# Layer pipeline on one core: TensorE's transposes and scores of a step set side by side, and all engines' operations reordered

## The reference, cut to what matters

```python
for i in range(DEPTH):                       # DEPTH = 6
    x = attn_layer(shift_tokens(x), Wqkv[i], q_scale[i], k_scale[i], Wo[i]) + x
    x = ffn_layer(shift_tokens(x), ln_g[i], ln_b[i], W1[i], b1[i], W2[i], b2[i]) + x
...
# attn_layer: 16 heads of 64, window 32 with one window of look-back
q = l2norm(q) * qs; k = l2norm(k) * ksc      # then rotary tables on both
sim = einsum('bhwie,bhwje->bhwij', bq, bk2) * 8.0; softmax over 64 keys; @ v; @ Wo
# ffn_layer: layer norm, a * gelu(gate) with 341 hidden features, W2
```

## Time and profile before

| | us |
|---|---|
| median of 3 runs | 1506.65 (1505.9 to 1509.11) |
| the profiled execution, its own time | 1507.59 |
| its span, first to last instruction | 1505.8 |
| TensorE busy / VectorE / GpSimd / ScalarE | 1441.7 / 1327.1 / 1209.8 / 1162.2 |

### The profile page before, as it was taken

How to read it: one execution, slowest core, us unless ns; L and a number is a source line. 1 busy time by engine, 2 the same in 40 slices (tenths; PEclk the granted TensorE clock), 3 DMA queues, 4 the chain that set the end, 5 groups by cost and what they waited for, 6 DMA issues and landing times.

```text
span 1505.8 us, 74802 instructions
## 1 busy us (share of the span) xinstructions
PE 1441.7 (96%) x32904; PEld 785.9 (52%) x32904; DVE 1327.1 (88%) x1789; ACT 1162.2 (77%) x2289; POOL 1209.8 (80%) x1051
## 2 busy tenths in 40 slices
PE   6877999999999999999999999999999999999985
PEld 6823444545545545545545545545555545545553
DVE  5478999989999989999999999989999999999974
ACT  4337888878888788888888888888888788888871
POOL 5148999878888888888888888888888888888841
PEclk9968999999999999999999999999999999999998
DMA  5100000020000020000020000020000000000000
GB/s 206 30 1 30 3 10 10 3 66 10 4 20 15 4 66 10 3 20 15 3 66 10 4 19 15 4 66 10 3 20 15 4 10 10 4 20 15 4 17 29
DMA packets 24564, 32.93 MB, mean 22 GB/s; under 512 B 2372, under 2 KB 21424, under 8 KB 23344
## 3 DMA queue, kind: packets, MB, share of 16 engines
q1 hardware_dynamic: 24240, 28.15, 5.8%
HBM read 20.80 MB, written 1.05 MB: 15 GB/s over the span
## 4 chain that ended last, share of the span: by engine, by line
PE 89%; DVE 5%; issue 2%; POOL 2%; ACT 1%; DMA 1%; SPq 0%; POOLq 0%; DVEq 0%; ACTq 0%
PE psq L257 22%; PE ring L279 21%; PE ring L309 11%; PE pss L298 9%; PE ring L267 9%; PE ring L323 8%; PE ring L333 4%; PE ring L346 1%; DVE qa L825 1%; PE ring L382 1%; DVE qb L841 1%; DVE mx L983 1%; DVE qb L961 1%; DMA xf<-x 0%; DMA mh<-in_bv 0%
## 5 line engine op out<-in xcount | busy, mean ns | idle before, releaser
L279 PE MATMUL ring<-mh,x0S 128*32 128x512 f32 x3072 | 407.9, 595 | 0.0
L257 PE MATMUL psq<-wqk,x0S 128*32 128x512 f32 x3072 | 394.9, 612 | 5.9 <-ACT sq L1200 4.9
L1332 POOL TENSOR_TENSOR qa<-qa,qb 128x1024 f32<-128x1024 f32 x96 | 229.2, 2388 | 6.7 <-DVE qb L961 6.7
L1391 POOL TENSOR_TENSOR qa<-qa,qb 128x1024 f32<-128x1024 f32 x96 | 228.6, 2382 | 0.0
L309 PEld LDWEIGHTS ring<-u,pT 128*32 128x32 f32 x6144 | 171.4, 111 | 61.8 <-issue 60.1
L309 PE MATMUL ring<-u,pT 128*32 128x128 f32 x6144 | 191.6, 274 | 4.1 <-DVE pT L978 4.1
L1373 POOL TENSOR_TENSOR pr<-pr,rden 128x1024 f32<-128x1024 f32 x96 | 183.9, 1916 | 12.8 <-DVE rden L860 12.8
L257 PEld LDWEIGHTS psq<-wqk,x0S 128*32 128x32 f32 x3072 | 93.6, 111 | 184.2 <-issue 168.4
L1352 POOL TENSOR_TENSOR qa<-qa,rn 128x1024 f32<-128x1024 f32 x96 | 182.7, 1903 | 0.2
L1368 POOL TENSOR_TENSOR qa<-qa,rn 128x1024 f32<-128x1024 f32 x96 | 182.8, 1904 | 0.0
L298 PEld LDWEIGHTS pss<-kT,qT 64*32 64x32 f32 x12288 | 134.8, 105 | 91.1 <-issue 83.6
(11 more groups left out here) (172 smaller groups left out, 2724.3 us busy)
## 6 DMA issues: line engine op xcount, KB each, us to landing
wqk<-in_wqk SPq DMA_DIRECT2D x6, 1024.0 KB, 8.6
mvT<-in_mvT SPq DMA_DIRECT2D x6, 512.0 KB, 3.8
wo<-in_wo SPq DMA_DIRECT2D x6, 512.0 KB, 5.2
xf<-x SPq DMA_DIRECT2D x24, 128.0 KB
xf<-x SPq DMA_DIRECT2D x24, 127.0 KB
rope<-in_rope SPq DMA_DIRECT2D x1, 2048.0 KB, 10.0
w<-in_w SPq DMA_DIRECT2D x6, 341.0 KB, 3.0
xmid<-in_x SPq DMA_DIRECT2D x4, 256.0 KB, 4.2
```

Source lines behind the costliest of these rows:

```text
L257: last = mm(psq[WIN * w:WIN * w + WIN, 512 * (n % 2):512 * (n % 2) + 512], x0S[:, tile * P + WIN * w:tile * P + WIN * w + WIN], wqk[:, l % ...
L279: last = mm(bank[WIN * g:WIN * g + WIN, :], x0S[:, tile * P + WIN * w:tile * P + WIN * w + WIN], mh[:, l % 2, g, :, :].rearrange("p j n -> ...
L1332: g_.tensor_tensor(qa[:, t % 2, 1024:2048], qa[:, t % 2, 1024:2048], qb[:, 1024:2048], ALU.add).then_inc(sum_k, 1)
L1391: g_.tensor_tensor(qa[:, t % 2, 0:1024], qa[:, t % 2, 0:1024], qb[:, 0:1024], ALU.add).then_inc(sum_q, 1)
```

## The change

Only orders and lags change; every operation, its operands, its semaphores and the waits in front of it stay as they are, but for the tile number that follows from the lag. In the table the tile numbers are those of step s; group operations, which stand in every fourth step, are in brackets with their lag.

| engine | before | after |
|---|---|---|
| TensorE | [G2 14], U3 s-5, U2 s-4, scores 1 s-4, q turn s-3, project q s-1, [A1 14], [F 12], mix 0 s-5, [G0 13], mix 1 s-5, [A0 13], U0 s-3, [Z 15], [A2 14], U1 s-3, [merge 8], [G1 13], project k s, [X 15], k turn s-2, scores 0 s-3 | [A2 15], mix 0 s-6, [G2 14], [G1 14], mix 1 s-6, U1 s-4, [X 16], U0 s-4, [A0 14], project k s-1, k turn s-3, q turn s-3, scores 0 s-4, scores 1 s-4, U2 s-4, U3 s-5, project q s-1, [F 12], [A1 14], [Z 15], [merge 8], [G0 13] |
| VectorE | subtract s-4, q product 1 s-1, [A1 14], q product 2 s-1, add x s-5, sum and reciprocal s-4, k squares' sum s-1, [A0 13], [statistics 9], [A2 14], [Z 15], q squares' sum s-1, k product 1 s, [aggregate 9], k product 2 s, small maximum s-1, transpose s-4, max s-3 | q squares' sum s-2, sum and reciprocal s-5, small maximum s-2, [A0 14], k product 1 s-1, k product 2 s-1, max s-4, transpose s-5, subtract s-4, q product 1 s-1, [statistics 9], q product 2 s-1, [Z 15], [aggregate 9], [A1 14], k squares' sum s-1, [A2 14], add x s-5 |
| ScalarE | [H 8], T0 and T1 s-2, [G2 13], U3 s-4, square k s, seed s-1, U2 s-3, T2 and T3 s-2, root's rest s-1, [F0 11], exp s-3, [G0 12], [F1 11], square q s, mask s-3, U0 s-2, U1 s-2, [xh 9], [G1 12], k look-back s-1, [X 14] | seed s-1, T0 and T1 s-2, root's rest s-1, square k s, T2 and T3 s-2, U2 s-3, U3 s-4, [xh 10], [F0, F1 11], exp s-3, [G0 12], [G2 12], [H 7], square q s, k look-back s-2, [G1 12], mask s-3, U1 s-2, [X 14], U0 s-2 |
| GpSimd | rb s-3, sum k s-2, rp and rn s-3, tables s, norm k s-3, norm q s-3, probabilities s-5, [group root 10], sum q s-2 | [group root 12], sum q s-4, rb s-4, probabilities s-7, tables s-2, rp and rn s-4, sum k s-3, norm q s-4, norm k s-4 |

The operations of the prologue's remainder move among these in the same way: the chunks' `chain_w` and `chain_d` now stand directly one behind the other, behind the k turn, behind U3 and at the end of the step, and the last `chain_d` of a step opens the next one. GpSimd's two layer norms of a unit go from lags 3 and 2 to 4. SyncE's program is not touched.

The core of the diff, TensorE's part:

```diff
             for s in range(STEPS + 20):
...
-                t = s - 4
-                if 0 <= t < STEPS:
-                    scores(t, 1).then_inc(s_ready, 1)
-                t = s - 3
-                if 0 <= t < STEPS:
-                    banks = [take("T2", t), take("T3", t)]
-                    pe.wait_ge(qn_q, t + 1)
-                    for bank, n in banks:
-                        wait(pe, freed[bank], n)
-                    turn([ring[bank] for bank, n in banks], t, 0)
...
-                t = s - 0
+                t = s - 1
                 if 0 <= t < STEPS:
...
                     wait(pe, sq_q, t)
                     project(t, 2)
                     project(t, 3).then_inc(pk_done, 1)
...
-                t = s - 2
+                t = s - 3
                 if 0 <= t < STEPS:
                     banks = [take("T0", t), take("T1", t)]
                     pe.wait_ge(qn_k, t + 1)
                     for bank, n in banks:
                         wait(pe, freed[bank], n)
                     turn([ring[bank] for bank, n in banks], t, 8)
...
                 t = s - 3
+                if 0 <= t < STEPS:
+                    banks = [take("T2", t), take("T3", t)]
+                    pe.wait_ge(qn_q, t + 1)
+                    for bank, n in banks:
+                        wait(pe, freed[bank], n)
+                    turn([ring[bank] for bank, n in banks], t, 0)
+                t = s - 4
                 if 0 <= t < STEPS:
...
                     pe.wait_ge(kprev_ready, t + 1)
                     scores(t, 0)
+                t = s - 4
+                if 0 <= t < STEPS:
+                    scores(t, 1).then_inc(s_ready, 1)
+                t = s - 4
+                if 0 <= t < STEPS:
+                    bank, n = take("U2", t)
+                    wait(pe, freed[bank], n)
+                    values(ring[bank], t, 2).then_inc(filled[bank], 1)
+                t = s - 5
+                if 0 <= t < STEPS:
+                    bank, n = take("U3", t)
+                    wait(pe, freed[bank], n)
+                    values(ring[bank], t, 3).then_inc(filled[bank], 1)
...
+                t = s - 1
+                if 0 <= t < STEPS:
+                    pe.wait_ge(sq_k, t + 1)
+                    project(t, 0)
+                    project(t, 1).then_inc(pq_done, 1)
```

More of the change, by code:

```diff
@@ L538, in _ @@
[L538 to L557, removed]
+                    hidden(ring[bank], 2, 0).then_inc(filled[bank], 1)
+                if chunk_at(s - 1, 0) >= 0:
+                    chain_d(chunk_at(s - 1, 0))
@@ new lines, in _ @@
+                if i >= 0:
+                    banks = [take("F0", i), take("F1", i)]
+                    pe.wait_ge(xh_ready, i + 1)
+                    for bank, n in banks:
+                        wait(pe, freed[bank], n)
+                    halves_turned([ring[bank] for bank, n in banks], lambda blk: xh[:, blk * P:blk * P + P], QUAD)
+                i = group_at(s, 14)
+                if i >= 0:
+                    bank, n = take("A1", i)
+                    wait(pe, freed[bank], n)
+                    hidden(ring[bank], 1, 0).then_inc(filled[bank], 1)
@@ new lines, in _ @@
+                i = group_at(s, 15)
+                if i >= 0:
+                    bank, n = take("Z", i)
+                    if i % GROUPS == 0:
+                        pe.wait_ge(w2_ready, 32 * (i // GROUPS + 1))
+                    abank, m = place["A2", i]
+                    pe.wait_ge(freed[abank], m + 1)
+                    wait(pe, freed[bank], n)
+                    narrow(ring[bank]).then_inc(filled[bank], 1)
+                i = group_at(s, 8)
+                if 0 <= i < LASTG:
+                    l, j = i // GROUPS + 1, i % GROUPS
+                    if j % 2 == 0:
+                        if j == 0:
+                            pe.wait_ge(mw_ready, 32 * (l + 1))
+                        merge((j, j + 1), l)
@@ new lines, in _ @@
+                i = group_at(s, 13)
+                if i >= 0:
+                    bank, n = take("G0", i)
+                    for r in range(2):
+                        nbank, m = place["F%d" % r, i]
+                        pe.wait_ge(freed[nbank], m + 1)
+                    if i % GROUPS == 0:
+                        pe.wait_ge(w1_ready, 16 * (i // GROUPS + 1))
+                    wait(pe, freed[bank], n)
+                    hidden(ring[bank], 0, 1).then_inc(filled[bank], 1)
+                if chunk_at(s - 1, 3) >= 0:
+                    chain_w(chunk_at(s - 1, 3))
@@ new lines, in _ @@
+                if chunk_at(s - 1, 1) >= 0:
+                    chain_W(chunk_at(s - 1, 1))
+                t = s - 5
+                if 0 <= t < STEPS:
+                    dve.wait_ge(p_ready, t + 1)
+                    if t >= 1:
+                        bank, n = place["Y", t - 1]
+                        dve.wait_ge(filled[bank], n + 1)
+                    v.transpose(pT[:, :, :].rearrange("p e n -> p (e n)"), pr[:, t % 2, :]).then_inc(pt_ready, 1)
+                if chunk_at(s - 1, 2) >= 0:
+                    chain_u(chunk_at(s - 1, 2))
@@ new lines, in _ @@
+                u = unit_at(s, 1)
+                if u >= 2:
+                    result(u)
+                if chunk_at(s, 0) >= 0:
+                    chain_u(chunk_at(s, 0))
+                i = group_at(s, 9)
+                if i >= 0:
+                    dve.wait_ge(bst_ready, i + 1)
+                    wait(dve, mrs_ready, i)
+                    for k in range(QUAD):
+                        last = v.bn_aggr(mv[:, k, :], bst[:, k, :])
+                    last.then_inc(mv_ready, 1)
```

664 lines of the change are left out of this document (302 added, 362 removed).

## The result

The change made the kernel slower: 1538.27 us (median of 4 runs, 1530.64 to 1550.14) against 1506.28 (4 runs, 1501.76 to 1509.11), a ratio of 1.0227 with an interval of 1.0164 to 1.029. The forecast was 1483, the range 1469 to 1500. The profiled execution took 1550.14 us, with a span of 1548.1.

The account below looks back on a forecast made before the run. TensorE's own matmul stream was taken as the bound: 35.5 us saved there less 12 us of new waits, 23.5 off 1507.59, gave 1484.1; with the profiled execution 0.9 above the median, 1483 us, range 1469 to 1500.

Parts of the forecast that it names:

- Nothing is added or left out on any queue: All queues: the change adds and removes no work, so TensorE alone comes out 35.5 us less.
- The three shape changes that fall away: TensorE's step: six changes of tile shape become three, saving 0.40 us a step, 38.4 us over 96 steps.
- The tight psq loop: Bank pair psq, shared by k and q: 0.37 us spare vanishes; rival that it takes most, 1492 to 1502, chance 0.20.
- My walk: Four-step count of TensorE and VectorE around psq: q projection waits 0.03, 0.14, 0.03 and 0.26 us, sum 0.46.
- classes 0 to 3: The four kinds of step by TensorE group work: F 0.53; G0, G2, G1, A0 3.44; A1, A2 1.72; Z, x transposes 3.17.
- ScalarE's squares as what is late next: q projection on psq: TensorE waits for ScalarE's squares, some 10 us in all; all waits together give back 12 us.
- VectorE at 90%: Sign of being right: VectorE's busy share near 90% of the span.
- GpSimd as the bound: Rival: both norm products, wanted at once, make the turns late; 1519 us at 0.5 us late a step, chance 0.07.
- The clock: Rival: turns and scores in one stretch drop TensorE to 1.2 GHz, 250 us more, 1756; chance 0.01.
- Joining the scores: TensorE: scores 1 directly behind scores 0 saves 0.13 us a step, taken between ends of 0 and 0.15.
- my sum: Whole kernel: 35.5 us gained on TensorE less 12 us of waits, 23.5 us off the profiled execution.
- costed the start at nothing within 3: Prologue and tail: lags tile against tile stay the same, so no cost, 3 us either way.

Follow-up runs that it names:

- aligned2: The changed kernel with 199 of its 576 projection and value parts run as two halves of 256 columns; 1498.96 us, 0.9945 against the kernel before.
- before_joined: The kernel before with one edit, scores 1 directly behind scores 0; 1533.06 us, 1.0193 against the kernel before.
- aligned: The changed kernel with 72 projection and value parts split into 256-column matmuls; 1505.67 us, 0.9994 against the kernel before.
- supply: The kernel before with 64 projection matmuls and four stretches of 1024 short matmuls behind its last TensorE instruction; ended 248 us after the kernel before.

## Why the prediction was wrong

**The step that failed** is "Nothing is added or left out on any queue", and behind it the sentence that TensorE works as long as its matmuls take. I counted the queues that the program writes and not the one that brings the program. The change adds no instruction, but it puts 320 of them into 2.6 us where before no block of 256 ran under 2.8. In the profiled execution the waits come to 53.5 us and the clock behind them to some 14 (before: 5.4 and 1.7), and no rival of mine contained it. The signs were there: half the scores take 0.79 us in the earlier trace rows, the page of before has the code queue, and its trace has three issue waits in the regular steps, all at a border.

**Point by point.**
- The three shape changes that fall away: right. The turns take 1.14 together, the q projection no longer has its 0.13, the scores 1.41 by the chain where I had 1.45. Their cover by other work held.
- The tight psq loop: right in size and kind. My walk had k to q at 6.20, 6.31, 6.20 and 6.43 in classes 0 to 3; in aligned2, where few stops are in the way, the medians from start to start are 6.18, 6.19, 6.18 and 6.42. From one k projection to the next, the shortest steps of the four classes in after are 11.92 (class 0), 14.87, 13.03 and 14.71 us, 54.5 together; my walk gave 11.92, 14.94, 13.11 and 14.79, together 54.8. In the kernel before they give 55.6.
- ScalarE's squares as what is late next: right in kind, too large in size, and not visible where I looked. I had forecast 12 us. The 3.7 us of waits of the psq matmuls for the squares belong to the early steps, and before has 5.2 of them, so they are no part of it. In the steady steps it is the weight load ahead of the matmuls that waits, as in the step of the chain above:

```profile
623.26 1.02 ACT L1117 ACTIVATE sq<-psq 128x1024 f32<-128x1024 f32 x1 [0.76 <-DVE qb L864]
...
624.34 0.16 PEld L257 LDWEIGHTS psq<-wqk,x0S 128*32 128x32 f32 x8 [0.78 <-ACT sq L1117]
624.34 1.92 PE L257 MATMUL psq<-wqk,x0S 128*32 128x512 f32 x16
```

  The squares end at 624.28, the first load goes at 624.34 and so no longer runs under the matmuls before it: the chain has 1.79 for this projection instead of 1.72. In 41 of the 43 steps of tiles 20 to 89 without a stop between k and q, the q projection starts within 0.15 us of the squares' end, and by the means of the four classes 0.03 to 0.08 us later behind the block ahead of it than where nothing holds it. At 0.06 in each of 96 steps that is an estimated 5 us.
- VectorE at 90%: wrong as a share (85%), because the span grew; its busy time fell from 1327.1 to 1313.3.
- GpSimd as the bound: the whole profile has one wait of a turn for it, of 0.3 us. The rival falls.
- The clock: I had named a granted clock under 0.97 as a sign of being wrong. It came at 0.972 (0.982 before), and the part that was lost was not lost by my route. Through turns and scores it stays at 1.00 (the window from 1186.60); it falls behind a stop. The Trainium skill (TensorE: Matmul & The Clock Gate, Part 4) has transposes not counting as activity; no run here shows the clock falling in the 1.14 us stretches of transposes alone.
- Joining the scores: my 0.13 can't be read alone. In the old order psq takes it back (before_joined); in the new one the whole step came out as summed.

The steps' gain is real, and aligned2 lets it be read: its profiled span is 16.4 us under that of before (1489.4 against 1505.8), where my sum had 23.5. The first scores start 2.3 us later (132.0 against 129.7), where I had costed the start at nothing within 3; from tile 0 to 20 it gains 10.0 (267.0 against 277.0), from tile 20 to 92 11.0 (1003.1 against 1014.1) and loses 2.3 in the tail. Where the 11.0 come from can be worked out further. Set each step from tile 20 to 92 against the shortest of its kind (its class, with or without a merge): the shortest steps add up to 988.2 us in aligned2 and 1009.4 in before, so undisturbed steps gain 21.2 in these 72, and my 23.5 over 96 was too low for them. But aligned2 exceeds its shortest steps by 15.1 us and before by 4.9. Of that, 6.3 and 3.1 are issue waits; 8.8 and 1.8 are lost while the view shows TensorE as busy. An example is the step that starts at 675.0 us: a border lies just ahead of its q projection, no idle time is shown, and the step is 0.51 longer than the shortest. How much of the 8.8 lies at borders is not shown, and why the start varies by 3 us between two executions stays open.

## What to carry to other kernels

Count instructions as well as columns: TensorE here took at most 256 in about 3.5 us when that was kept up, so matmuls that run at 11 ns each need slow ones around them, and putting all the short ones into one stretch can cost more than each shape change that it saves. A wait put down to "issue", in the middle of equal matmuls that need nothing new, is a reason to number the instructions and look at the number modulo 256. Then time and position in the stream matter together: an edit far ahead, or two matmuls of 256 columns for one of 512, can move a kernel by 3%, and two versions that differ in instruction count should not be compared on one alignment alone.

## What the runs showed that was not expected

- Code reaches TensorE in blocks of 16 KB during the run: 2.2 to 3.1 us from the start of the transfer to the first instruction of the block, 3.46 us a block in steady supply. The Trainium skill's page on the architecture (Trainium Architecture — The Big Picture, The software stack) has the instruction streams moved in at load; the 259 transfers of this trace are spread over the whole run.
- The next transfer mostly starts 0.1 to 1.2 us behind a border, sometimes shortly ahead of it. It came 2.0 to 3.4 us behind about half of the borders in projections in aligned, and 2.1 to 5.4 us behind borders around the layer loads.
- TensorE's clock was at the lower level for 3.4 or 6.8 us during or just behind 7 of the 33 stops in after; those seven lasted 1.8 to 3.8 us, and others of 2.1 us left the clock at 1.00. supply had 32 stops of up to 2 us and shows the lower level once behind them, for 6.8 us.
- Splitting a 512-column matmul in two of 256 adds no time where no border is in the way: aligned2 has 4448 instructions more and the same shortest steps (54.5 us for four), and its split projections take 1.84 and 1.75 us where the whole ones take 1.84 and 1.74.
